# Experts' weights split two slices a step from step 4 on; the third token group cut in two; expert-row scatters respread over the steps (attention and mixture of experts, 1 core)

## What is computed

```
x = x + tanh(g_xattn) * cross_attention(ctx, layernorm(x))     # softmax(q k^T) v, then @ Wfc
xf = layernorm(x)
gates = sigmoid(xf @ Wg)
vals, idx = top_k(gates, 2);  vals = vals / vals.sum(-1)
shared = silu(xf @ Ws1) * (xf @ Ws3) @ Ws2
h = silu(xf @ We1[e]) * (xf @ We3[e])
out = (shared + sum over the two chosen e of  w[t, e] * (h @ We2[e])) / 3
x = x + tanh(g_ffn) * out
```

## Time and profile before

| what | value |
|---|---|
| median of 3 runs (lowest to highest) | 450.26 us (449.73 to 450.26) |
| time of the profiled execution | 447.97 us |
| its span | 446.2 us |
| busy: PE, DVE, POOL, ACT | 79%, 77%, 63%, 59% |
| scatters L544, 64 | 63.9 us busy, mean 999 ns |
| PE's wait for the first expert rows | 11.55 us |

### The profile page before, as it was taken

The page is one execution under the profiler, slowest core; times in us unless marked ns, Lnnn a source line. Parts: engine busy times, 40 slices in busy tenths (PEclk is TensorE's granted clock), DMA queues, the critical chain, the costliest instruction groups (busy, mean ns, idle before and its releaser), DMA issues.

```text
span 446.2 us, 10643 instructions
## 1 busy us (share of the span) xinstructions
PE 354.7 (79%) x3712; PEld 266.4 (60%) x3712; DVE 341.5 (77%) x846; ACT 262.1 (59%) x598; POOL 279.3 (63%) x375
## 2 busy tenths in 40 slices
PE   0699999997998969899649943999999999999400
PEld 0366677675766638576537832777777777778200
DVE  2569999999999999999839831677776666667357
ACT  1257888886677846687524621556666555556244
POOL 4364666664579966888587771037777777777700
PEclk9999999999899988999958995999999999999955
DMA  3930699991011110000011714123336666631189
GB/s 103 282 88 3 256 394 388 399 391 35 25 32 45 37 49 25 27 27 25 26 38 48 267 54 132 49 71 96 90 117 230 232 229 228 237 145 49 51 276 294
DMA packets 39331, 62.36 MB, mean 140 GB/s; under 512 B 5936, under 2 KB 23344, under 8 KB 39280
## 3 DMA queue, kind: packets, MB, share of 16 engines
q1 hardware_dynamic: 32704, 51.12, 33.4%
q0 software_dynamic: 4992, 10.30, 6.9%
q10 hardware_dynamic: 1584, 0.27, 0.3%
HBM read 18.32 MB, written 31.56 MB: 112 GB/s over the span
## 4 chain that ended last, share of the span: by engine, by line
PE 39%; DVE 17%; issue 15%; POOL 14%; ACT 8%; DMA 5%; SPq 1%; DVEq 0%; POOLq 0%; ACTq 0%
POOL expert_rows L544 8%; PE ps L1221 6%; PE ps L1164 5%; PE ps L1223 5%; PE ps L1222 5%; POOL token_sums L624 3%; PE ps L1258 3%; DVE row_max L941 3%; PE ps L1118 3%; PE ps L1153 2%; DVE inv_sum L982 2%; PE ps L1183 2%; PE ps L1174 2%; ACT xT_hi L748 2%; PE ps L1200 1%
## 5 line engine op out<-in xcount | busy, mean ns | idle before, releaser
L624 POOL DMA_INDIRECT token_sums<-prob,y_at x92 | 94.3, 1025 | 60.2 <-DVE prob L1041 38.2
L544 POOL DMA_INDIRECT expert_rows<-c_sb,pos x64 | 63.9, 999 | 17.0 <-issue 17.0
L743 ACT ACTIVATE h_hi<-prob 128x512 fp32r<-128x512 f32 x62 | 38.3, 631 | 35.1 <-DVE prob L1004 35.1
L736 ACT ACTIVATE probT<-ps 128x512 f32<-128x512 f32 x62 | 37.0, 598 | 31.1 <-PE ps L1223 25.2
L586 POOL TENSOR_TENSOR k_mask<-k_st,head_mask 128x512 f32<-128x512 f32 x32 | 33.5, 1046 | 32.3 <-ACT k_st L699 32.0
L1118 PE MATMUL ps<-k_mask,qT 32*64 32x256 f32 x512 | 45.1, 424 | 8.5 <-DVE prob L947 7.8
L1004 DVE TENSOR_TENSOR prob<-ps,probT 128x512 f32<-128x512 f32 x62 | 40.5, 685 | 9.5 <-ACT probT L736 5.3
L941 DVE TENSOR_REDUCE row_max<-ps 128x16 f32<-128x1024 f32 x32 | 39.0, 1219 | 8.4 <-PE ps L1118 8.3
L1025 DVE TENSOR_TENSOR xT_lo<-ps,xT_hi 128x512 fp32r<-128x512 f32 x23 | 15.9, 692 | 35.9 <-ACT xT_hi L748 35.9
L1009 DVE TENSOR_TENSOR h_lo<-prob,h_hi 128x512 fp32r<-128x512 f32 x62 | 40.7, 689 | 3.1
L707 ACT ACTIVATE probT<-ps 128x512 f32<-128x512 f32 x64 | 35.1, 595 | 9.8 <-PE ps L1164 9.7
(11 more groups left out here) (164 smaller groups left out, 937.3 us busy)
## 6 DMA issues: line engine op xcount, KB each, us to landing
expert_rows<-zeros SPq DMA_DIRECT2D x36, 520.0 KB, 5.5
c_sb<-expert_rows SPq DMA_DIRECT2D x23, 260.0 KB, 2.7
wbuf_hi<-w_hi SPq DMA_DIRECT2D x15, 384.0 KB, 3.2
wbuf_lo<-w_lo SPq DMA_DIRECT2D x15, 384.0 KB, 3.7
w_raw<-in_L_ffn_We_dram SPq DMA_DIRECT2D x24, 128.0 KB, 4.1
c_sb<-token_sums SPq DMA_DIRECT2D x8, 256.0 KB, 5.1
xT_lo<-token_sums SPq DMA_DIRECT2D x8, 256.0 KB, 5.7
out_dram<-x_sb SPq DMA_DIRECT2D x8, 256.0 KB, 5.0
```

What stands on the lines that cost most here:

```text
L544: pool.indirect_dma_start(out=xs, out_offset=bass.IndirectOffsetOnAxis(pos[:, k, i:i + 1], 0), in_=c_sb[:, i, :], in_offset=None).then_inc ...
L624: pool.indirect_dma_start(out=ys, out_offset=bass.IndirectOffsetOnAxis(y_at[:, s, k:k + 1], 0), in_=yrows[:, s % 2, k * D:(k + 1) * D], in ...
```

## The change

Slices of the weights are split two in each step from step 4: steps 4 to 16 take two, step 17 the last one; a slice is 128 KB. SP issues one or two clears behind a refill in place of four, and five at the end. Group 16 to 24 becomes (16, 20) and (20, 24), with steps 26 to 29 and 30 to 33. `routing` takes the minimum of 1 + exp(-logit) in place of the maximum of its reciprocal, so that a group's reciprocal (L836) and its operation L841 are gone; `shares` gets two reciprocals of 128x32 and `slot_table` one small operation. Scatters are respread: two tiles in steps 26, 29, 31 and 34, one in the other steps from 18 to 37, tiles 24 to 31 in unit 0. PE's last counts (totals and `count_before`) move from the beginning of unit 1 to unit 0, between `up(1)` and `down(0)`; DVE's last `places` moves from the beginning of unit 1 to the end of unit 0.

```diff
-    WS_FROM = NT - 1 - SPLITS
+    WS_FROM = 4
-    GROUPS = [(0, 8), (8, 16), (16, 24), (24, 32)]
+    GROUPS = [(0, 8), (8, 16), (16, 20), (20, 24), (24, 32)]
-        def splits(t):
-
-            return not isinstance(t, int) or WS_FROM <= t < WS_FROM + SPLITS
+        def slices(t):
+
+            return range(max(0, 2 * (t - WS_FROM)), min(2 * (t - WS_FROM) + 2, SPLITS))
-        GATE_STEP = [14, 22, 30, None]
-        COUNT_STEP = [16, 24, 32, None]
-        RANK_STEP = [17, 25, 33, None]
+        GATE_STEP = [14, 22, 26, 30, None]
+        COUNT_STEP = [16, 24, 28, 32, None]
+        RANK_STEP = [17, 25, 29, 33, None]
...
-            if 18 <= t < NT:
+            if 18 <= t < 26:
                 return range(t - 18, t - 17)
-            return {NT: [14], NT + 1: [15], NT + 2: [16], NT + 3: [17], NT + 4: [18], NT + 5: [19]}.get(t, [])
+            return {26: [8, 9], 27: [10], 28: [11], 29: [12, 13], 30: [14], 31: [15, 16], 32: [17], 33: [18], 34: [19, 20],
+                    35: [21], 36: [22], 37: [23]}.get(t, [])
...
-                    for n in range(4 * (j - RING), 4 * (j - RING) + 4):
-                        if n < XALL // (P * ZROWS):
-                            clear_rows(n)
+                    for n in range(3 * (j - RING) // 2, 3 * (j - RING + 1) // 2):
+                        clear_rows(n)
+            for n in range(3 * (SPLITS - RING) // 2, XALL // (P * ZROWS)):
+                clear_rows(n)
...
-                if splits(t):
-                    pool.wait_ge(w_hi_ready, t - WS_FROM + 1)
-                    s = w_slice(t)
-                    pool.tensor_tensor(w_lo[:, s], w_raw[:, (t - WS_FROM) % RING, :], w_hi[:, s].bitcast(F32),
+                for j in slices(t):
+                    pool.wait_ge(w_hi_ready, j + 1)
+                    s = w_slice(j)
+                    pool.tensor_tensor(w_lo[:, s], w_raw[:, j % RING, :], w_hi[:, s].bitcast(F32),
                                        ALU.subtract).then_inc(w_split, 1)
...
                 if n == TAIL_UNIT:
-                    for i in range(20, 24):
-                        scatter(i)
-                if n == TAIL_UNIT + 1:
                     for i in range(24, 32):
...
-                if splits(t):
-                    s = w_slice(t)
-                    ring = (t - WS_FROM) % RING
-                    act.wait_ge(w_slice_in[ring], 16 * ((t - WS_FROM) // RING + 1))
-                    act.activation(w_hi[:, s], w_raw[:, ring, :], ACT.Copy).then_inc(w_hi_ready, 1)
+                for j in slices(t):
+                    s = w_slice(j)
+                    act.wait_ge(w_slice_in[j % RING], 16 * (j // RING + 1))
+                    act.activation(w_hi[:, s], w_raw[:, j % RING, :], ACT.Copy).then_inc(w_hi_ready, 1)
...
-                    then(dve.tensor_scalar(gt, gt, 1.0, None, ALU.add))
-                    then(dve.reciprocal(gt, gt))
-                    then(dve.tensor_reduce(top1[:, tiles], gt, AX_X, ALU.max))
+                    then(dve.tensor_scalar(gt, gt, 1.0, LARGEST, ALU.add, ALU.min))
+                    then(dve.tensor_reduce(top1[:, tiles], gt, AX_X, ALU.min))
...
-                    dve.tensor_scalar(c_sb[:, tiles, D + 1], rank[:, tiles], -1.0, float(E + 1), ALU.mult, ALU.add)
...
             def shares():
 
+                dve.reciprocal(top1[:, :], top1[:, :])
+                then(dve.reciprocal(top2[:, :], top2[:, :]))
...
                 if n == TAIL_UNIT + 1:
-                    places(NG - 1)
                     slot_table()
...
                 if n + 1 < UNITS:
                     hidden(n + 1)
+                if n == TAIL_UNIT:
+                    places(NG - 1)
...
             def unit(n):
-                if n == TAIL_UNIT + 1:
-                    pe.wait_ge(gate_exp, NG)
-                    pe.wait_ge(counted, NG)
-                    pe.matmul(p_totals, ones[:, :], carry[:, NG, :], start=True, stop=True).then_inc(totals_ready, 1)
-                    count_before(NG - 1)
...
                 if n + 1 < UNITS:
                     up(n + 1)
+                if n == TAIL_UNIT:
+                    pe.wait_ge(gate_exp, NG)
+                    pe.wait_ge(counted, NG)
+                    pe.matmul(p_totals, ones[:, :], carry[:, NG, :], start=True, stop=True).then_inc(totals_ready, 1)
+                    count_before(NG - 1)
```

More of the change, by code:

```diff
@@ L58, in gated_attention_and_experts @@
     NOWHERE = 1000.0
+    LARGEST = 1e38
     ZROWS = 8
@@ L74, in gated_attention_and_experts @@
     NHP = HEADS // 2
-    assert B % 2 == 0 and L == 64 and D == P and WALL % WSL == 0 and 0 < WS_FROM < 6 and T % ROWS == 0 and NT == 32
+    assert B % 2 == 0 and L == 64 and D == P and WALL % WSL == 0 and T % ROWS == 0 and NT == 32
     xt = x.rearrange("(t b) l d -> (b l) t d", b=2)
@@ L358, in xT_tile, with w_slice @@
             return flat[:, i * P:(i + 1) * P] if isinstance(i, int) else flat[:, bass.ts(i, P)]
-        def splits(t):
-            return not isinstance(t, int) or WS_FROM <= t < WS_FROM + SPLITS
-        def w_slice(t):
-            t = t - WS_FROM
-            return slice(t * WSL, (t + 1) * WSL) if isinstance(t, int) else bass.ts(t, WSL)
-        GATE_STEP = [14, 22, 30, None]
-        COUNT_STEP = [16, 24, 32, None]
-        RANK_STEP = [17, 25, 33, None]
+        def slices(t):
+            return range(max(0, 2 * (t - WS_FROM)), min(2 * (t - WS_FROM) + 2, SPLITS))
+        def w_slice(j):
+            return slice(j * WSL, (j + 1) * WSL)
+        GATE_STEP = [14, 22, 26, 30, None]
+        COUNT_STEP = [16, 24, 28, 32, None]
+        RANK_STEP = [17, 25, 29, 33, None]
         TAIL_UNIT = 0
@@ L821, in turned, with pick @@
                     return v[:, 0:E * m].rearrange("p (e t) -> p t e", e=E)
-                def pick(scores, top, picked):
+                def pick(scores, top, which, picked):
                     then(dve.tensor_tensor(key, scores, spread(top), ALU.is_equal))
                     then(dve.tensor_tensor(key, key, late, ALU.mult))
-                    then(dve.tensor_reduce(rank[:, tiles], key, AX_X, ALU.max))
-                    then(dve.tensor_tensor(picked, key, spread(rank[:, tiles]), ALU.is_equal))
+                    then(dve.tensor_reduce(which, key, AX_X, ALU.max))
+                    then(dve.tensor_tensor(picked, key, spread(which), ALU.is_equal))
                 if part == 0:
@@ L834, in routing @@
                     dve.wait_ge(gate_exp, g + 1)
-                    then(dve.tensor_scalar(gt, gt, 1.0, None, ALU.add))
-                    then(dve.reciprocal(gt, gt))
-                    then(dve.tensor_reduce(top1[:, tiles], gt, AX_X, ALU.max))
+                    then(dve.tensor_scalar(gt, gt, 1.0, LARGEST, ALU.add, ALU.min))
+                    then(dve.tensor_reduce(top1[:, tiles], gt, AX_X, ALU.min))
                 if part == 1:
-                    pick(gt, top1[:, tiles], pick1)
+                    pick(gt, top1[:, tiles], c_sb[:, tiles, D + 1], pick1)
                 if part == 2:
-                    dve.tensor_scalar(c_sb[:, tiles, D + 1], rank[:, tiles], -1.0, float(E + 1), ALU.mult, ALU.add)
-                    then(dve.scalar_tensor_tensor(out=gt2, in0=pick1, scalar=-4.0, in1=gt, op0=ALU.mult, op1=ALU.add))
-                    then(dve.tensor_reduce(top2[:, tiles], gt2, AX_X, ALU.max))
+                    then(dve.scalar_tensor_tensor(out=gt2, in0=pick1, scalar=2.0 * LARGEST, in1=gt, op0=ALU.mult,
+                                                  op1=ALU.add))
+                    then(dve.tensor_reduce(top2[:, tiles], gt2, AX_X, ALU.min))
                 if part == 3:
-                    pick(gt2, top2[:, tiles], pick2)
+                    pick(gt2, top2[:, tiles], rank[:, tiles], pick2)
                 if part == 4:
@@ L893, in slot_table @@
                                               in1=slot_less[:, :], op0=ALU.mult, op1=ALU.add))
+                then(dve.tensor_scalar(slot_late[:, :], slot_e[:, :], -1.0, float(E + 1), ALU.mult, ALU.add))
                 then(dve.tensor_tensor(slot_at[:, :], slot_at[:, :], slot_c[:, :], ALU.subtract))
```

3 lines of the change are left out of this document (2 added, 1 removed).

## The result

The kernel after is faster, by a third to two thirds of what was forecast. Beside its own runs of the kernel before it took 447.0 us (445.75 to 449.62, 7 runs) against 448.63; the recorded ratio is 0.9939 with a 95% interval of 0.9914 to 0.9965, the two medians alone make 0.9964, 1.6 us less. Run again later, with 12 runs against 29, it took 446.49 us against 449.94: 0.9924, interval 0.9895 to 0.9954. That is -3.4 us where -5.05 was forecast; both medians lie in the forecast's own range, 443 to 448.5.

A forecast was written before the change was run, and what follows sets the result against it. POOL's scatter queue bounds the kernel behind step 33, PE and ACT's ring steps 5 to 14, DVE the routed steps. 0.0 up to T31, -5.4 and +0.35 make -5.05: 445.3 us, own range 443 to 448.5, 8 in 10 440.8 to 450.2.

The forecast's parts named there:

- the ring: Steps 5 to 14: PE turns a tile, ACT works from xT_hi to tT, PE goes on; 5.55 us a turn.
- A: POOL becomes the pace of steps 26 to 31; slower, +0.7 us, 451.0; chance 0.12.
- B: About no change, within 0.2%: early steps cost their upper end, POOL hides less, gains at lower ends; chance 0.08.
- C: Larger gain, 441.3 us: step 29's excess and half the early steps' price absent, L827's whole 1.6 goes; chance 0.22.
- signs of being wrong: T14 not moved, T31 off by more than 3 us, or POOL without pause before the last group's scatters.
- Part 1: Steps 5 to 14: a second w_hi slice costs 0.30 us each turn over nine periods, +2.7.
- Part 2: Step 15: routing's reciprocal and L841 leave, -0.7, with +0.1 for catching up in steps 16 and 17.
- Parts 3 to 5: In order: T18 to T22 without slices -2.3; step 22 to 23, routing and clashes, -2.3; step 25, POOL earlier, -1.2.
- Part 6: Fifth group's routing behind steps 26 to 28: +1.4, +1.4, +0.1, step 28's own period -0.2; step 31's smaller group -0.9.
- Part 7: Two tiles a step: step 29's excess makes DVE wait for rstd in step 30, +1.9; hidden after 26 and 31.
- Part 8: Tail: last group's pos at 243.7, its 16 scatters from 243.8, the last at 263.0 instead of 268.43, -5.4.
- Part 9: shares gets two reciprocals, +0.74, partly taken in by the wait for ACT's copy: +0.35; slot_table's extra operation 0.

The follow-up runs named there:

- experiment 9: After with one tile in step 34 and slices spread from step 1 (two in 1 to 5, one in 6 to 14); 440.68 us, 0.9791.
- experiment 8: After with one tile in step 34 and step 29's second tile moved to step 27; 440.38 us, 0.9783.
- experiment 7: Kernel before with extra PE transposes in its routing steps 16, 17, 24 and 25; 449.62 against 450.57 us, 0.999.
- experiment 1: The changed kernel run again unchanged, for a second trace; 446.49 us, 0.9924.
- experiment 6: After with 8 to 20 extra PE transposes at the start of steps 16, 17, 24, 25, 28 and 29; 441.14 us, 0.9822.
- experiment 10: After with one tile in step 34, step 29's second tile in step 27, and the extra PE transposes; 436.40 us, 0.9694.
- experiment 11: After with step 34 at one tile, step 29's second tile in step 27, extra PE transposes and slices from step 1; 438.46 us, 0.9746.

## Why the prediction was right, and where its sizes were off

**Direction and mechanism held.** The gain is in the tail and in the routed steps, the price in the ring and behind step 29, as forecast. None of the rivals came true: not A (POOL the pace of six steps, slower than before), not B (within 0.2%), not C (441.3 us). But the total owes something to luck: three parts gained about 1 us more each than their terms, and a loss that was in no term took it back. Of the signs of being wrong that the prediction set, one appeared: T31 more than 3 us off 211.1. It was 215.63 us in the first trace, +4.53, and 212.38 in the second, +1.28.

**Part 1** (+2.7) was right in kind and nearly in size: T5 to T14 takes 52.19 us for 49.92, +2.27. The period from T5 to T6 stayed at 5.43 us, the eight others grew by 0.28 each, to 5.85 for a forecast 5.84, and experiment 9 takes it off again. That T14 is at 100.72 us for a forecast 100.64 is luck, with 0.51 us of T1 to T2 in it.

**Part 2** (-0.7) was too small: T14 to T15 lost 1.60 us. DVE's L825 had taken 1.00 us there beside `k_mask`, a block of 0.78; the trace of before shows it, and I had looked only at the reciprocal. The later T14 and the shorter chain together moved the block out of the way. That is luck of position: with the slices alone (experiment 2) it stands at L840 and 8.93 us remain, and the minimum alone (experiment 3) leaves 8.45, the forecast's own 8.43.

**Parts 3 to 5.** T18 to T22: 22.44 for 22.03, -1.9 us for -2.3 (the terms that part 3 names, three of 0.6 and one of 0.4, add up to 2.2). T22 to T23 lost 3.30 us for 2.3; L827's whole 1.6 went, not the half I gave it. T23 to T26 lost 2.1 us for 1.2 in one trace and in the experiment with PE kept busy, 1.3 in the other: in the best case not quite twice the part.

**Part 6** (+2.7) came out at T26 to T30: 25.55 and 25.23 us for 25.24 (second trace of after, and PE kept busy), where the first trace, with the fall of the clock, has 29.83. Inside it two errors cancel: T26 to T28 takes 15.1 and 15.2 us in the traces of after for a forecast 14.3, with L826's block of 1.2 us in place of the 0.3 given for a clash, and T28 to T30 10.4 us (again) for 11.0. The terms as written, 1.8, 1.5, 0.65 and 0.3 less 0.4 a step, make some 3.0 before step 28's -0.2, 0.1 more than the part has.

**Part 7** (+1.9 in step 30) was right in place and size, 1.79 us and 2.31 in the second trace, and experiment 8 removes 1.9 to 2.3 with it.

**Part 8** (-5.4) was -4.5 in the first trace. The row numbers were forecast 1.88 us later against T31 (243.7 - 211.1 = 32.6); they come at 248.01 + 0.17 - 215.63 = 32.55. The 16 scatters take 268.43 - 248.46 = 19.97 us for 19.2. The second execution loses another 1.5, all of it before tile 31's `rstd` (T31 + 22.34 us for + 20.89). PE has a lower clock there just behind T31, 0.82 over the 9.37 us from T31 where the first trace has 1.00:
```profile
212.38:221.75 9.37, 7.24 (x118) 6.12 (x114) 7.65 (x22) 3.12 (x7) 6.29 (x8) 0.82 0.10 32
```
That this is the cause was not tested.

**Part 9** (+0.35): the time from the last scatter to the end is 1.5 to 2.2 us longer than before in the two traces. About 0.6 of it is in the first three units behind the rows' arrival (13.42 us for 12.80). Experiments 2 and 7, without the two reciprocals, have 13.40 and 13.96 there, so the trace of before was a quick one, and the reciprocals' 0.35 can't be seen. A further 0.6 is a thing that I can't explain: from the tenth routed slot on, a unit takes 5.70 us in every kernel that routes by minimum, and 5.67 in every one that doesn't; PE's twelve matmuls of `up` take 2.87 us for 2.84. The cause was not looked for.

**The step that failed** is a term that isn't in the sum: PE's clock. I took each stretch's work at the durations of before, with its falls of the clock where they were, and asked only which wait ends last. Shortening DVE's and ACT's work in and around the routed steps moved PE's waits of 1.8 to 2.2 us to other steps, and the engine came back at 1.2 GHz, just when the others needed it. Against the kernel with PE kept busy this costs 2.2 to 2.5 us from T17 to T18 in both executions of after, and 4.6 from T26 to T30 in one of them, 0.3 in the other; from the ratios of experiments 1 and 6 it is 0.9924 - 0.9822 = 0.0102 of 450 us, 4.6 us, with the 0.72 us of DVE's block in it. Had it been absent, the forecast would have been too small: parts 2, 4 and 5 had 0.9 to 1.0 us each to spare, and after with PE kept busy gains 1.8%, 8 us.

The trace of before had it, and I passed it by: its windows from T15 to T16 and from T23 to T24 are not at full clock, and there too PE had waited for DVE's `prob`, 2.25 and 4.27 us.
```profile
107.03:114.86 7.83, 5.15 (x60) 3.79 (x48) 7.59 (x22) 3.58 (x9) 3.20 (x7) 0.82 0.07 17
161.55:168.17 6.62, 3.99 (x24) 2.17 (x25) 6.38 (x18) 2.29 (x5) 2.87 (x6) 0.62 0.13 40
```
```profile
109.66 0.66 PE L1118 MATMUL ps<-k_mask,qT 32*64 32x256 f32 x8 [2.25 <-DVE prob L947]
164.18 1.13 PE L1118 MATMUL ps<-k_mask,qT 32*64 32x256 f32 x8 [4.27 <-DVE prob L947]
```
In step 15 the fall costs nothing there: DVE has the routing to do, 7.59 of 7.83 us, and never waits for PE (experiment 7 takes the fall away and gains 0.04 us). After the change PE's wait of 1.82 us is a step later, and the fall meets step 17, in which DVE does wait for PE. The windows of after from T16 to T17 and from T17 to T18:
```profile
115.95:121.22 5.27, 3.02 (x67) 1.54 (x55) 5.24 (x17) 3.16 (x9) 1.83 (x4) 0.88 0.03 8
121.22:129.75 8.53, 8.53 (x99) 6.98 (x99) 7.00 (x21) 4.31 (x12) 4.63 (x8) 0.67 0.01 3
```
PE is busy 3.02 of 5.27 us, where before had 4.47 of 5.26 between the same starts, and then 8.53 of 8.53 us at a mean clock of 0.67.

What stays open: which executions lose the clock in steps 28 and 29; how much of the transposes' 1.0% is the clock's and how much a shift of DVE against POOL; the 5.70 us units; the price of the fifth group by itself, which no kernel tried; and the 4.7 us that PE still waits for the expert rows in the best kernel.

## What to carry to other kernels

When a change shortens the work of the engine that PE waits for, look for the stretches where PE will then stand idle just ahead of work that only PE can do, and price that work at the lower clock as one of the cases; cheap transposes into unused PSUM are a quick test of it, and here they were worth 1.0% in the changed kernel and nothing in the old one. A second unit of queue work in a step can cost its whole length where the next wait on that queue is near (2.5 us in step 34, about 2 of 2.56 in step 30); that it is free where the wait is far, as the forecast had it for steps 26 and 31, no run tried by itself: place it by the next thing that the queue has to deliver. And an operation that takes several times its usual time beside another engine's is not bound to its line; count it as one block that will be somewhere, or nowhere, and keep both ends.

## What the runs showed of the hardware that I had not expected

The granted clock differs between executions of one program at the same place: 0.53 and 1.00 from 195 to 206 us. What a fall costs depends on what it meets: nothing in step 15 of the kernel before, 2.2 to 2.5 us from T17 to T18 and 3.8 from T29 to T30 in the kernel after. It may be most of the spread of this program's runs: the kernel of experiment 10 has a spread of 1.8 us over 6 runs, after has 5.2 over 12, but that of experiment 11, with the same transposes, has 3.7 over 6. That is a reading of spreads, not a test.

A DVE operation of 128x32 with two SBUF inputs took 1.39 us beside `k_mask`, seven times its usual 0.19; of the operations that DVE's timelines of before and after list singly none took 0.2 us over its median with nothing but a scatter beside it, and DVE did little to them, three of after's 64 taking more than 1200 ns:
```profile
L547 POOL DMA_INDIRECT expert_rows<-c_sb,pos x64: 954/958/1435, 135.1 to 268.4; - x64
```
With more of them moved into DVE's busy steps the median is still 958 ns and the shortest 954, as in the earlier trace rows. These are the times of GpSimd's instruction; from issue to landing such a DMA took 2.4 us in the median.
